# A two-layer perceiver block: the second layer's three stages merged tile by tile, with the inverse-scale product on GpSimd

## The reference, cut to what matters

```python
x = x + L0_xattn(ctx, ctx, norm(x), mask)   # cross attention, 16 heads, 1024 keys a batch, masked
x = x + L0_attn(norm(x))                    # causal linear attention
x = x + L0_ffn(norm(x))                     # feed-forward, int8 fake quantisation
x = x + L1_xattn(norm(x), ctx, ctx)         # cross attention, 16 heads, no mask
x = x + L1_attn(norm(x))                    # causal softmax attention over the 64 rows of a batch
x = x + L1_ffn(norm(x))                     # gated feed-forward of width 704, FP4 quantisation
```

## Time and profile before

| what | us |
|---|---|
| median of three runs | 1435.48 |
| the profiled execution | 1439.74 |
| its span in the trace | 1437.8 |
| PE / DVE / ACT / POOL busy | 1300.0 / 939.4 / 784.8 / 656.6 |
| mean granted TensorE clock | 0.955 of full speed |

### The profile page before, as it was taken

How to read it: one execution, slowest core, us unless ns; L and a number is a source line. 1 busy time by engine, 2 the same in 40 slices (tenths; PEclk the granted TensorE clock), 3 DMA queues, 4 the chain that set the end, 5 groups by cost and what they waited for, 6 DMA issues and landing times. The chain is left out here.

```text
span 1437.8 us, 27154 instructions
## 1 busy us (share of the span) xinstructions
PE 1300.0 (90%) x10721; PEld 895.3 (62%) x10722; DVE 939.4 (65%) x1670; ACT 784.8 (55%) x1315; POOL 656.6 (46%) x351
## 2 busy tenths in 40 slices
PE   6999999999999966965599999999999997897697
PEld 3676676666666644642256666766667665696465
DVE  4656655666556755957657768676566566586886
ACT  4675666666666623534366666666666664354311
POOL 2755566656666522400145556565555555440200
PEclk9999999999999988987699999999999998899798
DMA  4221111211111030000210100200010000000000
GB/s 159 76 58 45 45 45 45 87 47 45 45 45 45 1 102 0 1 1 0 108 37 31 51 30 31 80 31 31 31 59 31 31 1 24 4 1 1 0 11 19
DMA packets 17085, 55.29 MB, mean 38 GB/s; under 512 B 2753, under 2 KB 8897, under 8 KB 12737
## 3 DMA queue, kind: packets, MB, share of 16 engines
q1 hardware_dynamic: 16960, 53.56, 11.4%
HBM read 52.51 MB, written 1.05 MB: 37 GB/s over the span
## 5 line engine op out<-in xcount | busy, mean ns | idle before, releaser
L429 POOL TENSOR_TENSOR ca_prob<-ca_prob,ca_inv_sum 128x1024 f32<-128x1024 f32 x256 | 493.4, 1948 | 378.4 <-DVE ca_inv_sum L707 378.4
L608 ACT ACTIVATE ca_kT<-bank,ca_bk 64x512 f32<-64x512 f32 x256 | 174.6, 682 | 223.4 <-PE bank L465 221.6
L512 PEld LDWEIGHTS bank<-ident,ca_prob 128*128 128x128 f32 x2048 | 238.4, 141 | 89.4 <-issue 65.7
L512 PE MATMUL bank<-ident,ca_prob 128*128 128x128 f32 x2048 | 266.7, 274 | 9.0 <-POOL ca_prob L429 7.0
L465 PE MATMUL bank<-ca_ctxT,ca_wk 128*128 128x512 f32 x512 | 244.4, 602 | 17.4 <-DMA ca_bk<-in_L_xattn_bk 17.4
L477 PE MATMUL bank<-ca_wv,ca_ctxT 128*128 128x256 f32 x1024 | 254.5, 392 | 0.0
L684 DVE CUSTOM_DVE_ANT_0 ca_neg_logit<-bank,ca_mask_add 128x1024 f32<-128x1024 f32 x128 | 151.6, 1222 | 131.6 <-PE bank L502 95.0
L477 PEld LDWEIGHTS bank<-ca_wv,ca_ctxT 128*128 128x128 f32 x1024 | 184.6, 190 | 82.2 <-issue 62.5
L687 DVE TENSOR_REDUCE ca_neg_max<-bank 128x1 f32<-128x1024 f32 x128 | 150.7, 1219 | 103.3 <-PE bank L502 103.3
L630 ACT ACTIVATE ca_prob<-ca_neg_logit,ca_neg_max 128x1024 f32<-128x1024 f32 x128 | 146.9, 1150 | 62.8 <-DVE ca_neg_max L684 62.8
L630 ACT ACTIVATE ca_prob<-bank,ca_neg_max 128x1024 f32<-128x1024 f32 x128 | 142.5, 1114 | 63.8 <-DVE ca_neg_max L687 63.8
(11 more groups left out here) (278 smaller groups left out, 1333.9 us busy)
## 6 DMA issues: line engine op xcount, KB each, us to landing
ca_ctxT<-in_ctxT SPq DMA_DIRECT2D x32, 1024.0 KB, 5.0
ca_mask_i<-in_mask SPq DMA_DIRECT2D x32, 256.0 KB, 6.4
lat<-in_x SPq DMA_DIRECT2D x1, 1024.0 KB, 4.9
out<-lat SPq DMA_DIRECT2D x8, 128.0 KB, 1.9
la_w_qkv<-in_L_attn_w_qkv SPq DMA_DIRECT2D x1, 768.0 KB, 3.9
la_w_down<-in_L_ffn_w_down SPq DMA_DIRECT2D x1, 704.0 KB, 8.0
ca_fw_raw<-in_L_ffn_w_down SPq DMA_DIRECT2D x1, 704.0 KB, 4.3
la_w_gate<-in_L_ffn_w_gate SPq DMA_DIRECT2D x1, 640.0 KB, 5.7
```

Of the source, the lines that this page charges most:

```text
L429: pool.tensor_tensor(prob[:, x, :], prob[:, x, :], inv_sum[:, x:x + 1].broadcast_to([P, CTX]), ALU.mult).then_inc(norm_ready, 1)
L512: tr = pe.transpose(bank[:, x, n * P:(n + 1) * P], prob[:, 2 * (s % 2) + p, (4 * h + n) * P:(4 * h + n + 1) * P], core.ident[:, :])
L608: op = act.activation(kT[half * S:(half + 1) * S, b % 2, 2 * m + r, :], bank[r * S:(r + 1) * S, x, :], ACT.Identity, bias=bk[r * S:(r + 1) ...
```

## The change

The second layer becomes one block, `second_layer`. Its loop goes over the steps of the cross attention and 18 more (`END` = 82). A tile t whose cross attention is finished at step 10 + 8t goes on in the following steps: `tile_at(s, lag)` gives the tile that is `lag` steps behind this point, if there is one. Lags 1 to 8 are the causal attention (`CausalTiles`), lags 9 to 15 the feed-forward (`Fp4Tiles`). Norms are taken for two tiles at once (`TileNorm`): the one for the attention of tile j and the one for the feed-forward of tile j-1. All products take banks 4 to 7 in turn (`Banks.open`).

The causal attention takes scores only within a batch: 64 queries' rows of two heads by 64 keys, on the upper and lower 64 rows of the array, so that its probabilities are 128 x 1024 instead of 128 x 2048. Its distances to the maximum move from VectorE to GpSimd. In the feed-forward of a tile GpSimd multiplies by the inverse scales (`divide_hidden`) and by the scales (`scale_hidden`), and VectorE does the seven other instructions in two parts, one step apart.

The quantisation of the three weights moves to the first layer's cross attention (VectorE from steps 4, 20, 36 on, one instruction a step), followed there by the product with the scales on GpSimd, 36 transposes on TensorE in nine groups, and 18 copies on ScalarE. The mask buffer of layer 0 is single, the queries are held for half of the batches at a time, the second half of the queries is projected in steps 28 and 29 (before: 8 and 12). The linear attention and the int8 feed-forward are as they were.

The core of the diff, in the order of the new file (all lines are new; those of the old functions that they replace are left out):

```diff
+    def scale_on_pool(self, pool, x):
+        pool.wait_ge(self.step, 8 * (x + 1))
+        grid, scale = fp4_scaled(self.raw[:, 0:self.blocks[x] * HD], self.scale[:, 0:self.blocks[x]], self.blocks[x])
+        pool.tensor_tensor(grid, grid, scale, ALU.mult).then_inc(self.scaled, 1)
...
+    def open(self, pe, key, bank=None):
+        if bank is None:
+            bank = 4 + self.turn % 4
+            self.turn += 1
+        wait(pe, self.taken[bank], self.count[bank])
+        self.count[bank] += 1
+        self.at[key] = (bank, self.count[bank])
+        return bank
...
+FW_STEPS = (4, 20, 36)
...
+                for x in range(3):
+                    if 10 <= s - FW_STEPS[x] < 13:
+                        ffn_weights.transposes_on_tensor(pe, x, s - FW_STEPS[x] - 10)
...
+                for x in range(3):
+                    if s == FW_STEPS[x] + 8:
+                        ffn_weights.scale_on_pool(pool, x)
...
+        x = [self.banks.open(pe, ("ss", t, g)) for g in range(2)]
+        for m in range(KD):
+            for j in range(2):
+                for c in range(2):
+                    for g in range(2):
+                        rows = slice(S * g, S * (g + 1))
+                        o = (4 * m + 2 * j + c) * S
+                        mm = pe.matmul(self.core.bank[:, x[g], o:o + S], self.q4[rows, m, c, 2 * j:2 * j + 2, :],
+                                       self.qk[rows, 1, m, c * S:(c + 1) * S], start=True, stop=True,
+                                       tile_position=(S * g, 0))
...
+        x = [self.banks.open(pe, ("so", t, c)) for c in range(2)]
+        for hc in range(4):
+            for j in range(4):
+                head = 4 * hc + j
+                m, g, pair, e = head // 8, head % 8 // 4, head % 4 // 2, head % 2
+                for c in range(2):
+                    rows = slice(S * c, S * (c + 1))
+                    mm = pe.matmul(self.core.bank[32 * j:32 * j + 32, x[c], hc * S:(hc + 1) * S],
+                                   self.value[rows, head, :], self.probT[rows, g, 2 * m + pair, e * S:(e + 1) * S],
...
+        scrambled = self.cat[:, :].rearrange("p (r u) -> p u r", u=4)
+        for u in range(4):
+            for c in range(2):
+                rows = slice(S * c, S * (c + 1))
+                mm = pe.matmul(self.core.bank[rows, x, 0:D], scrambled[rows, u, :], self.w_o[rows, u, :],
+                               start=(u == 0), stop=(u == 3), tile_position=(S * c, S * c))
+        self.banks.done(mm, ("sy", t))
...
+    def quantise_hidden(self, dve, t, part):
+        if part == 0:
+            for a in range(2):
+                self.banks.wait_taken(dve, ("fu", t, a))
+            dve.wait_ge(self.x_ready, t + 1)
+        steps = fp4_steps(self.hid[:, :], FB, self.mag[:, :], self.scale[:, :], self.inv[:, :], self.hid[:, :],
+                          self.e[:, :])
+        if part == 1:
+            dve.wait_ge(self.h_step, 8 * t + 4)
+        for n in range(4 * part, 3 + 5 * part):
+            steps[n](dve).then_inc(self.h_step, 1)
+            dve.wait_ge(self.h_step, 8 * t + n + 1)
+    def divide_hidden(self, pool, t):
+        pool.wait_ge(self.h_step, 8 * t + 3)
+        hid, inv = fp4_scaled(self.hid[:, :], self.inv[:, :], FB)
+        pool.tensor_tensor(hid, hid, inv, ALU.mult).then_inc(self.h_step, 1)
+    def scale_hidden(self, pool, t):
+        pool.wait_ge(self.h_step, 8 * (t + 1))
+        grid, scale = fp4_scaled(self.hid[:, :], self.scale[:, :], FB)
+        pool.tensor_tensor(grid, grid, scale, ALU.mult).then_inc(self.h_ready, 1)
...
+def tile_at(s, lag):
+    n = s - 10 - lag
+    return n // 8 if n >= 0 and n % 8 == 0 and n // 8 < TILES else None
...
+            for s in range(END):
+                if s < STEPS:
+                    ca.scores(pe, s)
+                if (t := tile_at(s, 4)) is not None:
+                    sa.scores(pe, t)
+                if s % 2 == 0 and 4 <= s < STEPS + 3:
+                    ca.times_v(pe, s // 2 - 2)
+                if (t := tile_at(s, 7)) is not None:
+                    sa.heads(pe, t)
+                if (t := tile_at(s, 8)) is not None:
+                    sa.output(pe, t)
+                if s + 2 < STEPS:
+                    ca.project_v(pe, s + 2)
+                if (t := tile_at(s, 2)) is not None:
+                    sa.project(pe, t)
+                if (t := tile_at(s, 6)) is not None:
+                    sa.transposes(pe, t, 0)
+                if (t := tile_at(s, 10)) is not None:
+                    ff.latent_transposes(pe, t)
+                if (t := tile_at(s, 11)) is not None:
+                    ff.project(pe, t, 0)
+                if (t := tile_at(s, 14)) is not None:
+                    ff.hidden_transposes(pe, t)
+                if 1 <= s <= STEPS:
+                    ca.transposes(pe, s - 1, 0)
+                if (t := tile_at(s, 6)) is not None:
+                    sa.transposes(pe, t, 1)
+                if s + 4 < STEPS:
+                    ca.project_k(pe, s + 4)
+                if (t := tile_at(s, 7)) is not None:
+                    sa.back(pe, t)
+                if (t := tile_at(s, 11)) is not None:
+                    ff.project(pe, t, 1)
+                if (t := tile_at(s, 15)) is not None:
+                    ff.down(pe, t)
+                if 1 <= s <= STEPS:
+                    ca.transposes(pe, s - 1, 1)
+                if s in Q_STEPS:
+                    ca.project_q(pe, 1, Q_STEPS.index(s))
+                if (t := tile_at(s, 1)) is not None:
+                    sa.latent_transposes(pe, t, attn_xn)
+                if (t := tile_at(s, 0)) is not None:
+                    if t == 0:
+                        pe.wait_ge(ca.wo_loaded, 32)
+                    ca.output(pe, t)
...
+            for s in range(END):
+                if (t := tile_at(s, 2)) is not None:
+                    sa.spread_queries(pool, t)
+                if s < STEPS:
+                    ca.normalise(pool, s)
+                if s % GROUPS == 2 and s // GROUPS + 1 < B:
+                    ca.queries(pool, s // GROUPS + 1)
+                if (t := tile_at(s, 4)) is not None:
+                    sa.distances(pool, t)
+                if (t := tile_at(s, 12)) is not None:
+                    ff.divide_hidden(pool, t)
+                if (t := tile_at(s, 13)) is not None:
+                    ff.scale_hidden(pool, t)
...
+            for s in range(END):
+                if s < STEPS:
+                    ca.exponentials(act, s)
+                if (t := tile_at(s, 5)) is not None:
+                    sa.exponentials(act, t)
+                if (t := tile_at(s, 7)) is not None:
+                    sa.take_heads(act, t)
+                if (t := tile_at(s, 2)) is not None:
+                    sa.take_queries_and_keys(act, t)
+                if (t := tile_at(s, 6)) is not None:
+                    sa.take_transposed(act, t)
+                if (t := tile_at(s, 10)) is not None:
+                    ff.take_latents(act, t)
+                if (t := tile_at(s, 14)) is not None:
+                    ff.take_hidden(act, t)
+                if (t := tile_at(s, 11)) is not None:
+                    ff.silu(act, t)
+                if s + 4 < STEPS:
+                    ca.take_k(act, s + 4)
+                if 1 <= s <= STEPS:
+                    ca.take_t_on_scalar(act, s - 1, 1)
+                if s == Q_STEPS[0]:
+                    ca.take_q_on_scalar(act, 1)
+                if (t := tile_at(s, 1)) is not None:
+                    sa.take_latents(act, t)
+                if s >= 10 and s % 8 == 2 and (s - 10) // 8 <= TILES:
+                    norm.root_on_scalar(act, (s - 10) // 8)
...
+            for s in range(END):
+                if s < STEPS:
+                    ca.maxima(dve, s)
+                if s >= 11 and s % 8 == 3 and (s - 11) // 8 <= TILES:
+                    norm.finish_on_vector(dve, (s - 11) // 8, (attn_free, ffn_free))
+                if (t := tile_at(s, 4)) is not None:
+                    sa.logits(dve, t)
+                if s % 2 == 0 and 4 <= s < STEPS + 3:
+                    ca.take_pv(dve, s // 2 - 2)
+                if (t := tile_at(s, 8)) is not None:
+                    sa.take_output(dve, t)
+                if s + 2 < STEPS:
+                    ca.take_v(dve, s + 2)
+                if (t := tile_at(s, 2)) is not None:
+                    sa.take_value(dve, t)
+                if 1 <= s <= STEPS:
+                    ca.take_t_on_vector(dve, s - 1, 0)
+                if (t := tile_at(s, 6)) is not None:
+                    sa.take_transposed_on_vector(dve, t)
+                if s < STEPS:
+                    ca.inverses(dve, s)
+                if (t := tile_at(s, 7)) is not None:
+                    sa.divide(dve, t)
+                if (t := tile_at(s, 11)) is not None:
+                    ff.hidden(dve, t)
+                if (t := tile_at(s, 9)) is not None:
```

(24 more changed lines are left out.)

1645 lines of the change are left out of this document (822 added, 823 removed).

## The result

The changed kernel takes 1479.55 us (median of four runs, 1479.03 to 1485.18) where the kernel before takes 1436.47 beside it: a ratio of 1.031, 95% interval 1.028 to 1.034. The profiled execution has a span of 1476.7, against 1437.8.

A forecast was written before the change was run, and what follows sets the result against it. TensorE was taken to bound the kernel. Span 1437.8 - 225.7 + 184.5 + 75 + 5 - 2.5 = 1474 us, carried over to a median of 1471; range 1402 to 1508, likeliest case 1450 to 1490.

The forecast's parts named there:

- The period: Eight steps of layer 1's merged loop: 89.1 us, 29.0 over before, as VectorE and GpSimd hold each other up.
- rival 1: Exclusion between VectorE and GpSimd costs nothing in layer 1's loop: six periods lose 6.0 each, 1436 us; chance 0.16.
- rival 2: Bank rotation absorbs VectorE's lateness in layer 1's loop, TensorE keeps its pace: period 78.4, 1404 us; chance 0.20.
- One sign: Predicted trace evidence: TensorE idle ahead of transposes for `ca_v` in steps of lag 2 and lag 6.
- Lag 2: Layer 1 steps at lag 2 and 10: input quantisation delayed by GpSimd's normalising products, 13.9 us.
- the walk: Step-by-step costing of one eight-step period in layer 1: 83.1 without exclusion, 18.3 work and 4.7 waiting over 60.1.
- Lag 6: Layer 1 steps at lag 6 and 14: normalising products get between VectorE's hidden-tile instructions; 13.4 to 15.1, taken 14.3 us.
- The sum: Time added to layer 1's cross attention from step 10: 8.7, five periods 145.0, last piece 30.8; together 184.5 us.
- the 2.5 of layer 1's weight steps: VectorE's weight quantisation steps leaving layer 1 for layer 0: 2.5 us taken off the span.
- the net of 5: Layer 0's extra work against what leaves layer 1: +5.4 - 2.5 + 2.5 = 5 us.
- The end: From layer 1's last product with V to the kernel's end, tiles 6 and 7 finishing: 75 us in all.
- Layer 0: Moved weight work in its cross attention: transposes 4.4, waits 1, VectorE's weight steps 2 to 3; other engines nothing.

The follow-up runs named there:

- e1_short_normalise: Changed kernel with GpSimd's normalisation in layer 1 cut to the first 128 of 1024 columns, the rest left unnormalised: 1423.2 us, ratio 0.990.
- e4_divide_on_vector: Changed kernel with the hidden values' product by inverse scales moved back from GpSimd to VectorE: 1478.2 us, ratio 1.029.
- e12_best_again: Changed kernel, reordered: GpSimd does scale_hidden, queries (lags 4, 12) and distances before normalising; VectorE quantises x before inverses. Repeat with more runs: 1430.2 us, ratio 0.995.
- the better order: Block order of e12_best_again, against the changed kernel's order: 1430.2 us; with the product by inverse scales back on VectorE 1434.8 us.

## Why the prediction came out right, step by step

**The period.** 89.1 against 88.9, and each step within 1.5. That VectorE and GpSimd shut each other out was the deciding assumption, and it stands: rival 1, where it costs nothing, wanted lags 2 and 6 at 10.8 and 11.4; rival 2, where the rotation of banks absorbs VectorE's debt, wanted 78.4. One sign came out otherwise than written: in lag 2 and lag 6 TensorE waits not for `ca_v` but for the bank of the product with V (2.37) and for GpSimd's hidden product (2.59); the wait for `ca_v` stands in lag 1. Lag 2 was predicted with waits of 1.8 and 1.5 for the scale and the multiplication; they took 1.65 and 1.78 where 0.18 and 0.43 are their own. The Trainium skill's rule (SBUF — State Buffer, section Who interferes with whom) and the traces agree; the rows above show moreover that products queued on GpSimd get in between two VectorE instructions one at a time.

**What cancels.** The sum of the period is closer than the walk behind it. Without GpSimd's long products the walk gave 83.1, and e1_short_normalise measures 79.4: it was 3.7 too long, 1.5 of that in lag 6 and 0.7 in lag 2. What GpSimd costs was put at 6.0, 3.1 in lag 2 and 2.9 in lag 6; it is 9.5, namely 2.8, 5.9 and another 0.8 in lag 1. The mechanism is the one predicted, but that the two errors nearly cancel is luck.

**Lag 6** was mis-sized: 14.3 taken, 13.4 to 15.1 as its bounds, 15.8 measured. VectorE's part was right (maxima at 6.5, predicted 7.0; GpSimd's product done at 7.9, predicted 8.4). What the walk lacked is TensorE's clock behind its wait of 2.59. The view by stretch of step 56, up to that wait's end and from there, and under them step 48 of e4_divide_on_vector, whole:

```profile
1294.40:1302.38 7.98, 5.39 (x85) 3.93 (x84) 7.57 (x6) 2.68 (x5) 5.62 (x4) 1.00 0.01 2
1302.38:1310.20 7.82, 6.79 (x31) 4.86 (x31) 4.09 (x8) 4.09 (x10) 1.94 (x2) 0.78 0.00 0
...
1205.13:1218.92 13.79, 10.68 (x116) 7.37 (x115) 11.23 (x13) 6.76 (x14) 6.52 (x4) 1.00 0.00 1
```

In the second stretch the clock is granted at 0.78: the eight transposes there take 1.93, the four of the causal weights 1.06 and K 2.31. In step 48 of e4_divide_on_vector, which stays at 1.00 behind a like wait of 2.08, they take 1.18, 0.65 and 1.88, and the step lasts 13.79. In all other tiles of that kernel from step 24 on the clock over this step is 0.79 or 0.89 and it lasts 15.4 to 16.6. So the clock costs lag 6 about 2 us, and without that loss it would lie within the forecast's bounds.

**The sum.** Five periods: 151.5 more instead of 145.0. Four of them are within 1.1 of the forecast (the first, 90.1, holds a lag 2 of 14.16 at a clock of 0.88); the one with the second half of the queries (steps 26 to 33) is 95.1. I had put those projections at nothing, or 1 to 2; they add 1.7, 2.2, 1.3 and 0.9 to lags 2, 3, 4 and 6 there, and the 3.4 that steps 8 and 12 lost against before were not in the sum either. Steps 10 to 17 take 67.4 (predicted 68.8), the last piece 74.1 (75.5).

**The time.** The span was forecast at 1474 and is 1476.7. It is nearer than its terms: the sum takes the 2.5 of layer 1's weight steps off twice, once within the net of 5 and once more for the span. The median was forecast at 1471 and is 1479.55, and most of these 8.5 us come from the step between the two: the profiled execution of the kernel before lay 4.3 above its median, that of the changed kernel 0.5 below it. The two lengths of the last section, some 5 us apart, would explain that, but no trace of the other runs shows it.

**The end** was 80.8 instead of 75. Up to gate and up of tile 6 it agrees (13.5 against 13.9). The hidden chain of tile 6 then mixes with the logits and maxima of tile 7 on VectorE, and its transposes end at 36.2 instead of 33.2; and its down product takes 5.21, not 2.8, at a granted clock of 0.53 (0.69 over the whole end). The pieces by the chain that ended last:

```profile
1409.48 7.10 PE bank L1784 x16
...
1436.20 5.21 PE bank L1806 x12
...
1451.05 6.82 PE bank L1784 x16
...
1468.39 4.71 PE bank L1806 x12
```

I had counted that product at full clock. The forecast's own pieces up to the sum of tile 7's attention add up to 42.2, not 42.4; measured are 47.9. From there to the end it agrees (32.9 against 32.6).

**Layer 0** hides behind a misleading number: step 63 of its cross attention comes 5.8 us later, of which 5.3 arise between steps 0 and 63. Layer 1 still began only 1.1 later because the profiled execution won 4.7 back in between, by its clock (last section). In e12_best_again, whose clock in that stretch was nearly as in before, layer 1 begins at 738.38, 5.6 later. The forecast's terms for layer 0 were 5.4 for the transposes with their waits and 2 to 3 for the weight steps, nearer 8; the net of 5 had already taken off what leaves layer 1.

**Prices.** The causal attention's half-array products lay near or below my low ends of 1.9, 1.7 and 1.0: scores 1.93 for 32 instructions (taken: 2.5), output 1.94 for 16 (2.2), heads 0.86 for 64 (2.0), in the timelines. That won little, since lags 1, 2 and 6 are set by VectorE. The change of ScalarE's table costs 1.28, as in the earlier trace rows; the timeline of step 53 shows SiLU right behind it:

```profile
1270.49 0.19 ACT L568 ACTIVATION_READ_ACCUMULATOR ca_prob<-bank,ca_neg_max 128x1 f32 x1
1270.70 1.28 ACT L1824 ACT_TABLE_LOAD   x1
1271.99 0.82 ACT L1824 ACTIVATE ca_ff_hid<-bank 128x352 f32<-128x352 f32 x2
```

Between the load's end and SiLU's start there is 0.01 us, and before the load 0.02, so the drain of 1.38 us that the Trainium skill adds (ScalarE: Activation LUTs, section What ACT_TABLE_LOAD costs) does not appear, and lag 3 came out at 11.8 without it.

**The named product.** The prediction gave GpSimd's product by inverse scales no gain or loss of its own in the period; in the written order the kernel with it on VectorE is 1.4 us faster, less than can be told, and in the better order 4.5 slower.

## What to carry to other kernels

Where VectorE and GpSimd both work from SBUF, the order of the blocks is a price of its own: try VectorE's chains of short SBUF instructions before the instruction that releases a long GpSimd product, and on GpSimd do first what ends VectorE's chain. Here that was worth 49 us of 1480 with no work removed, and it turned a loss of 3% into a gain of 0.5%. Before shifting a whole stage by a step, list for every step what its chains would then meet; a merge also has to be sized with the clock that TensorE keeps after each wait it adds.
